# A graph layer with one-hot sums: column numbers read from PSUM, a gathered block's sums in another bank, group one-hots in 16-bit pairs

## What is computed

```
out_deg = jnp.maximum(segment_sum(ones, src, N), 1.0)
in_cnt  = segment_sum(ones, dst, N)
t1  = feat @ W1
msg = t1[src] + feat[src] * feat[dst] @ W2
msg = msg / (jnp.sqrt(out_deg[src]) * jnp.sqrt(out_deg[dst]))[:, None]
agg = segment_sum(msg, dst, N)
embed = leaky_relu(where(in_cnt > 0, t1 + agg, 0) + b, 0.01)
embed = embed / jnp.maximum(norm(embed, axis=1), 1e-12)
out = layernorm(x + embed)
```

## Time and profile before

| | |
|---|---|
| time, median of 3 runs | 1109.14 us (1108.18 to 1111.76) |
| the profiled execution's own time | 1105.97 us |
| its span in the profile | 1104.1 us |
| TensorE busy (matmul) | 927.1 us, 84% |
| VectorE busy | 722.0 us, 65% |
| GpSimd busy | 684.5 us, 62% |
| ScalarE busy | 480.1 us, 43% |
| gathers (L681) | 616, first at 208.9 us, last at 1055.8 us |

### The profile page before, as it was taken

How to read it: one execution, slowest core, us unless ns; L and a number is a source line. 1 busy time by engine, 2 the same in 40 slices (tenths; PEclk the granted TensorE clock), 3 DMA queues, 4 the chain that set the end, 5 groups by cost and what they waited for, 6 DMA issues and landing times.

```text
span 1104.1 us, 31256 instructions
## 1 busy us (share of the span) xinstructions
PE 927.1 (84%) x13011; PEld 819.3 (74%) x13011; DVE 722.0 (65%) x1523; ACT 480.1 (43%) x1357; POOL 684.5 (62%) x651
## 2 busy tenths in 40 slices
PE   3376650299899999999999999999999999999893
PEld 2265540278788888888888888888888888888782
DVE  8999999835366555566566566656556567467443
ACT  5899967423233333333334333334333333333311
POOL 4400000377777777777777777777777777777720
PEclk9985555589999999999999999999999999999997
DMA  9100004655555545555555555555555555555520
GB/s 313 59 2 1 2 2 177 229 148 146 158 154 165 161 142 165 153 161 164 164 147 163 165 159 162 164 166 155 164 160 154 167 159 158 159 157 167 152 82 21
DMA packets 68120, 155.83 MB, mean 141 GB/s; under 512 B 12006, under 2 KB 37668, under 8 KB 67972
## 3 DMA queue, kind: packets, MB, share of 16 engines
q0 software_dynamic: 40144, 123.12, 39.4%
q1 hardware_dynamic: 27828, 30.65, 8.5%
HBM read 137.69 MB, written 16.03 MB: 139 GB/s over the span
## 4 chain that ended last, share of the span: by engine, by line
POOL 52%; issue 18%; DVE 13%; PE 13%; DMA 2%; ACT 0%; POOLq 0%; DVEq 0%; ACTq 0%
POOL y_rows L681 52%; PE g_ps L814 6%; DVE hi_hot L329 4%; DVE lo_hot L338 3%; PE emb_ps L852 2%; DVE xs L420 2%; PE grp_ps L776 2%; DMA y_rows<-y_parts,idx_tab 1%; DVE yp L406 1%; PE win_ps L795 1%; DMA yp<-in_spans_dram,widx 1%; DVE yp L305 1%; PE hist_ps L510 1%; DMA y_parts<-yp 0%; DVE yp L412 0%
## 5 line engine op out<-in xcount | busy, mean ns | idle before, releaser
L681 POOL DMA_INDIRECT y_rows<-y_parts,idx_tab x616 | 660.5, 1072 | 192.6 <-issue 185.5
L814 PE MATMUL g_ps<-yp,counts 128*128 128x256 bf16 (+1 forms) x4410 | 571.4, 274 | 0.0
L814 PEld LDWEIGHTS g_ps<-yp,counts 128*128 128x128 f16 x4410 | 408.6, 98 | 49.4
L710 ACT CAST counts<-win_ps 128x392 f16<-128x392 f32 x480 | 230.4, 484 | 465.0 <-PE win_ps L795 463.6
L923 DVE TENSOR_TENSOR key_hot<-iota_h,pairs 128x1568 f16<-128x1568 f16 x120 | 116.9, 974 | 279.8 <-PE win_ps L795 278.4
L795 PE MATMUL win_ps<-key_hot,lo_hot 128*128 128x98 f16 x1920 | 168.7, 211 | 50.8 <-DVE lo_hot L923 49.8
L795 PEld LDWEIGHTS win_ps<-key_hot,lo_hot 128*128 128x128 f16 x1920 | 131.3, 100 | 71.5 <-DVE lo_hot L923 50.8
L923 DVE TENSOR_TENSOR lo_hot<-iota_h,pairs 128x2048 f16<-128x2048 f16 x120 | 146.8, 1223 | 37.2 <-PE win_ps L795 36.3
L776 PEld LDWEIGHTS grp_ps<-hot,y_rows 128*128 128x128 bf16 x3696 | 104.0, 97 | 39.6 <-DMA y_rows<-y_parts,idx_tab 37.4
L776 PE MATMUL grp_ps<-hot,y_rows 128*128 128x48 bf16 x3696 | 108.0, 184 | 30.2 <-DMA y_rows<-y_parts,idx_tab 30.0
L445 ACT ACTIVATE yp<-iota_b,half_lo 128x128 bf16<-128x128 bf16 x416 | 122.3, 402 | 0.8 <-PE step_ps L510 0.8
(11 more groups left out here) (123 smaller groups left out, 668.4 us busy)
## 6 DMA issues: line engine op xcount, KB each, us to landing
y_rows<-y_parts,idx_tab POOLq DMA_INDIRECT x616
y_parts<-yp SPq DMA_DIRECT2D x6, 1344.0 KB, 5.1
xs<-in_x_dram SPq DMA_DIRECT2D x1, 6144.0 KB
xb<-in_x_dram SPq DMA_DIRECT2D x48, 128.0 KB
out_dram<-o_sb SPq DMA_DIRECT2D x48, 128.0 KB
src_i<-in_src_t_dram SPq DMA_DIRECT2D x1, 784.0 KB, 5.1
y_parts<-yp SPq DMA_DIRECT2D x1, 768.0 KB, 4.3
y_parts<-yp SPq DMA_DIRECT2D x1, 576.0 KB, 5.5
```

The source lines that it names most:

```text
L681: nc.gpsimd.indirect_dma_start(out=y_rows[:, g % RING, t, :], out_offset=None, in_=y_dram[:, :], in_offset=bass.IndirectOffsetOnAxis(ap=id ...
L710: nc.scalar.copy(counts[:, c % 2, :, i * WN:(i + 1) * WN], win_ps[:, i % 2, 0:KEYS].rearrange("p (d s) -> p s d", s=BLOCKS)).then_inc(s_cn ...
L814: last = nc.tensor.matmul(g_ps[:, c % 2, 0:n], counts[:, c % 2, s, :], yp_1[:, s, m * D:m * D + n], start=(s == 0 and m == PARTS - 1), sto ...
```

## The change

Three edits belong together. The row of column numbers is copied once into a PSUM bank (`iota_w`, read as 16-bit `iota_ps`), and the main part's three one-hots (`key_hot`, `lo_hot`, `hot`) compare against that copy in place of `iota_h` and `iota_f` in SBUF. The bank comes from `g_ps`: a gathered block's turned sums now stand in columns 192 and up of the groups' bank `grp_ps`, where before they had a bank of their own; so a block may be turned only when no group's sums are unread there (a wait on `s_acc`), and a group may start only when the block's sums have been read (a wait on `s_uv`). The slots of the groups are moved so that none stands in the six slots from `at` on. And `hot` is now made from 16-bit inputs in pairs: `rel` holds each number twice, which costs a second subtraction in setup; `iota_f` and its copy are gone.

```diff
-        rel = sb("rel", [P, GT], F16)
+        rel = sb("rel", [P, GT, 2], F16)
...
-                    nc.vector.tensor_copy(iota_f[:, :], iota_i[:, 0:W])
...
+                        for k in range(2):
+                            nc.vector.tensor_tensor(rel[:, :, k].rearrange("p (g t) -> p g t", t=TILES),
+                                                    dst_f[:, :].rearrange("p (g t) -> p g t", t=TILES),
...
-            g_ps = ps2("g_ps", [P, 3, 512])
+            g_ps = ps2("g_ps", [P, 2, 512])
+            iota_w = ps2("iota_w", [P, 512])
+            iota_ps = iota_w[:, :].bitcast(F16)
...
+            for b in range(BG):
+                at = gathered_from(b)
+                for g in range(GROUPS):
+                    if at <= slots[g] < at + SUMS_AFTER + 2:
+                        slots[g] = at + SUMS_AFTER + 2
+                    if g >= 1:
+                        slots[g] = max(slots[g], slots[g - 1] + 3)
...
                         if g >= 1:
                             pe.wait_ge(s_acc, g)
-                        at = (g % 2) * GW
+                        read = [end_of[0, b] for b in range(BG) if gathered_at[b] < slots[g]]
+                        if read:
+                            pe.wait_ge(s_uv, read[-1] + 1)
+                        at = 0
...
+                        pe.wait_ge(s_acc, sum(slot <= gathered_at[b] for slot in slots))
                         for h in range(H):
-                            nc.tensor.transpose(g_ps[:, 2, h * P:(h + 1) * P], gb[:, h, :], ident[:, :])
+                            nc.tensor.transpose(grp_ps[:, GAT + h * P:GAT + (h + 1) * P], gb[:, h, :], ident[:, :])
...
-                        nc.vector.tensor_tensor(hot[:, g % 2, :, :],
-                                                iota_f[:, 0:W].unsqueeze(1).to_broadcast([P, TILES, W]),
+                        nc.vector.tensor_tensor(
+                            hot[:, g % 2, :, :].rearrange("p t (c two) -> p t c two", two=2),
+                            iota_ps[:, 0:W].rearrange("p (c two) -> p c two", two=2).unsqueeze(1)
...
-                            iota_h[:, 0:cols].rearrange("p (c two) -> p c two", two=2).unsqueeze(1)
+                            iota_ps[:, 0:cols].rearrange("p (c two) -> p c two", two=2).unsqueeze(1)
...
+                    nc.vector.tensor_copy(iota_w[:, 0:P // 2], iota_h[:, :].bitcast(F32)).then_inc(s_iotap, 1)
+                    dve.wait_ge(s_iotap, 1)
```

More of the change, by code:

```diff
@@ L105, in build @@
         ones_b = sb("ones_b", [P, 1], BF16)
-        iota_f = sb("iota_f", [P, W], F32)
         iota_h = sb("iota_h", [P, P], F16)
@@ L350, in gather_tables @@
                         nc.vector.tensor_scalar(base_i[0:1, :], near[0:1, :], float(P), float(NEAR * P), ALU.max, ALU.min)
[L351 to L354, removed]
+                        for k in range(2):
+                            nc.vector.tensor_tensor(rel[:, :, k].rearrange("p (g t) -> p g t", t=TILES),
+                                                    dst_f[:, :].rearrange("p (g t) -> p g t", t=TILES),
+                                                    base_ps[:, 0:GT // TILES].unsqueeze(2)
+                                                    .to_broadcast([P, GT // TILES, TILES]), ALU.subtract)
                         link(nc.vector.tensor_scalar(in_reach[:, :], near[0:1, 0:GROUPS], float(P), float(NEAR * P),
@@ L608, in build @@
             s_out = [sem("s_out0"), sem("s_out1")]
+            GAT = 192
             CW = H * W
@@ L620, in build @@
             ALL = PRODUCTS + PIECES
+            ACC_AFTER = 3
+            SUMS_AFTER = 4
+            slots = [FIRST_SLOT + g * SLOTS_A_GROUP[0] // SLOTS_A_GROUP[1] for g in range(GROUPS)]
             def group_slot(g):
[L623 to L628, removed]
+                return slots[g]
             def last_group(j):
@@ L637, in gathered_from @@
                 return at + (WB // 2 - at) % WB
+            for b in range(BG):
[5 more added lines that the diff above has]
+                        slots[g] = max(slots[g], slots[g - 1] + 3)
+            assert all(b > a for a, b in zip(slots, slots[1:]))
+            gathered_at = [gathered_from(b) for b in range(BG)]
+            assert not any(at <= slot < at + SUMS_AFTER + 2 for at in gathered_at for slot in slots)
+            group_at = {group_slot(g): g for g in range(GROUPS)}
+            hot_at = {(group_slot(g - 1) + 1 if g else 0): g for g in range(GROUPS)}
+            acc_at = {group_slot(g) + ACC_AFTER: g for g in range(GROUPS)}
             ends = sorted([((d + 2) * WB, DENSE, d) for d in range(BD)] + [(gathered_from(b), 0, b) for b in range(BG)])
@@ L827, in turn_sums @@
                             pe.wait_ge(s_uv, end_of[0, b - 1] + 1)
+                        pe.wait_ge(s_acc, sum(slot <= gathered_at[b] for slot in slots))
                         for h in range(H):
-                            nc.tensor.transpose(g_ps[:, 2, h * P:(h + 1) * P], gb[:, h, :], ident[:, :])
-                        nc.tensor.matmul(g_ps[:, 2, D:D + 1], cb[0:1, :], ones_f[0:1, 0:1],
+                            nc.tensor.transpose(grp_ps[:, GAT + h * P:GAT + (h + 1) * P], gb[:, h, :], ident[:, :])
+                        nc.tensor.matmul(grp_ps[:, GAT + D:GAT + D + 1], cb[0:1, :], ones_f[0:1, 0:1],
                                          start=True, stop=True).then_inc(s_g0, 1)
@@ L880, in one_hots @@
                             dve.wait_ge(s_grp, g - 1)
[L881 to L884 removed]
+                        nc.vector.tensor_tensor(
+                            hot[:, g % 2, :, :].rearrange("p t (c two) -> p t c two", two=2),
+                            iota_ps[:, 0:W].rearrange("p (c two) -> p c two", two=2).unsqueeze(1)
+                            .to_broadcast([P, TILES, W // 2, 2]),
+                            rel[:, g * TILES:(g + 1) * TILES, :].unsqueeze(2).to_broadcast([P, TILES, W // 2, 2]),
+                            ALU.is_equal).then_inc(s_hot, 1)
                     def accumulate(g):
@@ L898, in accumulate @@
                             dve.wait_ge(s_near, j)
-                        of = (g % 2) * GW
                         at = gT[:, (j % 2) * H:(j % 2) * H + H, bass.ds(base, W)]
-                        nc.vector.tensor_tensor(at, at, grp_ps[:, of:of + CW].rearrange("p (h w) -> p h w", h=H), ALU.add)
+                        nc.vector.tensor_tensor(at, at, grp_ps[:, 0:CW].rearrange("p (h w) -> p h w", h=H), ALU.add)
                         at = cnt[0:1, j % 2, bass.ds(base, W)]
-                        nc.vector.tensor_tensor(at, at, grp_ps[0:1, of + CW:of + GW], ALU.add).then_inc(s_acc, 1)
+                        nc.vector.tensor_tensor(at, at, grp_ps[0:1, CW:GW], ALU.add).then_inc(s_acc, 1)
                     def move_on(j):
@@ L943, in sums @@
                             dve.wait_ge(s_uvT, n)
[L944 to L947, removed]
+                        g_in = g_ps[:, b % 2, :] if k == DENSE else grp_ps[:, GAT:]
+                        nc.vector.tensor_copy(degrees[:, n:n + 1], g_in[:, D:D + 1])
+                        nc.vector.tensor_scalar(has[:, e:e + 1], g_in[:, D:D + 1], 0.0, None, ALU.is_gt)
+                        nc.vector.scalar_tensor_tensor(out=uv[:, 0, :], in0=g_in[:, 0:D],
                                                        scalar=rs[:, at:at + 1], in1=xb[:, e, :],
                                                        op0=ALU.mult, op1=ALU.add)
-                        nc.vector.scalar_tensor_tensor(out=uv[:, 1, :], in0=g_ps[:, of, 0:D],
+                        nc.vector.scalar_tensor_tensor(out=uv[:, 1, :], in0=g_in[:, 0:D],
                                                        scalar=rs[:, at:at + 1], in1=xb[:, e, :],
@@ L1016, in _ @@
                             one_hots(hot_at[u])
-                        for n in ends_due(u, 4):
+                        for n in ends_due(u, SUMS_AFTER):
                             sums(n)
```

1 line of the change is left out of this document (added).

## The result

The changed kernel takes 1077.61 us (median of 4 runs, 1075.87 to 1077.94), against 1108.66 us before (4 runs): the ratio is 0.9718, 95% interval 0.9686 to 0.975, 31 us less. The forecast was 1082 us, the range 1070 to 1099. The profiled execution has a span of 1076.2 us, 27.9 less than before; it is this difference that the traces have to explain.

The account below looks back on a forecast made before the run. GpSimd's own pace, 1.38 us a gather, was taken as the bound, with TensorE close behind. Terms -33 - 8.5 + 9 + 0.7 + 5 = -27 us, taken from the 1109.14 us median, gave 1082 us; range 1070 to 1099.

Parts of the forecast that it names:

- What holds a gather up: GpSimd's gathers: VectorE instructions with two SBUF inputs stretch those starting inside them, 80.2 us in all.
- Who is bound then: Main part after the change: TensorE becomes the bound and GpSimd waits for the ring.
- Waits for rows: TensorE's weight loads waiting for gathered rows: of 37.4 us, 4 kept, so -33 us.
- Clock: TensorE's half-clock stretches after long waits: five of six go at 1.7 us each, -8.5 us; bounds 0 and -10.
- Reading PSUM: VectorE's one-hots with one input in PSUM, hot now in pairs: about nothing in all.
- rival A: VectorE's comparison from PSUM runs at 1.02 ns a column, not 0.52, slower: 1142 us, chance 13%.
- Accumulation waits: TensorE, groups three slots apart: 13 waits of 0.6 us for VectorE's accumulation plus 1, +9 us; bounds 0 and 25.
- Rival C: TensorE's new waits eat more, 25 in place of 9 us, with half the clock gain: 1103 us, chance 8%.
- Moved groups: 27 groups up to six slots, 7 us, later; GpSimd has up to four groups in hand, so nothing charged.
- Setup: Setup on VectorE: second rel subtraction costs 0.80 us, the iota_f copy (0.18 us) goes, +0.7 us.
- Rest: Stretched gathers that stay and pile-ups of two or three groups on the ring of four: +5 us.

Follow-up runs that it names:

- E1: Changed kernel with all three one-hots comparing with iota_h in SBUF again; slots, bank, pairs and the copy into PSUM stay: 1110.69 us, ratio to before 1.0001.
- E2: Changed kernel with only the group one-hot (hot) reading iota_h in SBUF again: 1077.21 us, ratio to before 0.9699.
- E3: Changed kernel with only the group one-hot reading PSUM; key_hot and lo_hot read SBUF again: 1111.07 us, ratio to before 1.0005.
- E5: Changed kernel with lo_hot alone reading iota_h in SBUF again; key_hot and hot read PSUM: 1086.28 us, ratio to before 0.9774.
- E4: Changed kernel with VectorE's accumulation of a slot put ahead of key_hot or lo_hot of the same slot: 1067.4 us, ratio to before 0.9613.
- E7: Kernel with the accumulation ahead (1067.4 us), its group one-hot not in pairs and one subtraction in setup: 1067.3 us, ratio to before 0.96.
- E6: Changed kernel with key_hot alone reading iota_h in SBUF again; lo_hot and hot read PSUM: 1081.21 us, ratio to before 0.9729.

## Why the prediction was right, step by step

The mechanism was right and the sum good to 1 us (-27 against -27.9), but partly by luck: the gain from rows was put 5.7 us too high, and 5 us were charged for a rest that cost nothing.

- **What holds a gather up.** Shown by E1 to E3: the same instructions at the same durations (1223 and 1222 ns) stretch gathers from SBUF and not from PSUM. The Trainium skill, "SBUF — State Buffer", section "Who interferes with whom", says that a VectorE instruction with two SBUF inputs contends with a GpSimd instruction that reads SBUF, and one with a single SBUF input outside the two-port modes does not; these runs agree for the gathers (667.0 us in E1, 586.8 in the change). Two things in my reading were off. The count of 162 gathers inside an L923, 149 stretched, does not come out of the start stamps, which give 201 and 170. And an instruction with two SBUF inputs is not the only kind that holds gathers: five gathers before started inside a copy of `cnt` right ahead of a one-hot and lost 5.5 of the 80 us.
- **Who is bound then.** TensorE, as predicted. It has the chain, and GpSimd waits for it; in E5 the two paces about cross, and TensorE still has the chain.
- **Waits for rows, -33 us: too large.** I took the weight loads' 37.4 us. The matmuls' own idle time is closer to what the end sees: 30.0 us before, 2.7 after, -27.3. With that row the sum closes (below).
- **Clock, -8.5 us: -10.2.** All six stretches went, also that at 1029.6, 6 x 1.7 us. This and the row term are TensorE's side of one change of bound, not two gains: E1 and E3 differ by two such stretches and not in time.
- **Reading PSUM, nothing: right.** 970 and 1222 ns rule rival A out. `hot` takes 347 ns, where I had 405: the 45 ns that I added for PSUM from the fp32 rows don't exist, and 160 + 384 x 0.52 = 360 would have been the better sum. The tier table of the Trainium skill's "VectorE: DVE Perf Modes", by which A would hold, does not fit these rows; the text under it does.
- **Accumulation waits, +9 us: place, count and mechanism right.** 13 waits of 0.54 us shown, where I had 0.56. Their cost is about 0.70 each by E4, 8.8 in all, and 0.7 for one `turn_sums`; E4 gets 10.2 back. Rival C's 25 did not come: the longest is 0.6 us.
- **Moved groups, nothing: right.** TensorE has no wait for rows after 303 us, and from 650 us on GpSimd waits for the ring, so it has the lead that I counted on.
- **Setup, +0.7 us: 0.9 to 1.7.** The first gather starts at 210.5 us (208.9 before); in the other kernels with two subtractions it is 209.8 to 210.6, with one (E7) 209.1.
- **Rest, +5 us: nothing.** The 6.5 us of stretches that stay (most of them, 4.3, inside L938, L1011, L1002 and L1026, which read and write SBUF alone) lie on GpSimd, which has slack. Here I charged to the path what stands on an engine with slack.

In measured terms: -27.3 (rows), -10.2 (clock), +7.7 (matmul idle for accumulations: 7.0 and 0.7), +1.6 (setup) = -28.2, against -27.9 of span; with E4's 8.8 us for the 13 waits in place of 7.0 it is -26.4.

## What to carry to other kernels

When one engine stretches the instructions of another, look at which instruction the stretched ones start inside and where its operands lie; moving one small constant operand from SBUF to PSUM removed the contention here for one PSUM bank and at no cost to the reader, 1223 against 1222 ns. Before counting the gain, ask whose pace is next: the contention cost GpSimd 87 us (E1), and taking it away gave 33, since from then on TensorE's own pace counts, so that a partial cure (E6) was nearly as good as the whole. And when two users of one buffer come closer together, move the reader that frees it ahead of whatever it stood behind: that one reordering was worth 10 us more.

## What was unexpected of the hardware

- A one-hot with both inputs in SBUF holds a gather that starts inside it, and not one that has already begun: 0.12 us earlier, and the gather ran its 0.95 us beside it (E1). A copy inside SBUF also held gathers that had begun up to half a microsecond before: one that began 0.40 us ahead of it took 1.13 us (E1).
- The 16-bit pair rate holds with one input in PSUM: 384 columns take 347 ns in pairs and 548 ns without (E7).
- Stretches nearly add. `lo_hot` alone costs the gathers 58.4 us (E5), `key_hot` alone 38.9 (E6, 619.2 - 580.3), both with `hot` 86.7 (E1); over the 6.5 us that the change keeps these are 51.9, 32.4 and 80.2, so the two alone sum to 84.3.
- A wait that the trace puts at 0.54 us for matmuls and 0.79 for their weight loads moved the next work by 0.70 us.
